# A two-layer attention and mixture-of-experts kernel: the end of each attention group put in another order, and the first expert's weight parts made at other places

## The chip, the cores and the metric

The kernel runs on one core of a Trainium2 chip. The metric is the device time of the whole program in microseconds; lower is better. Engines are called by the names of the profile: PE is TensorE, DVE is VectorE, ACT is ScalarE, POOL is GpSimd, SP is SyncE, which here only issues DMAs.

## What is computed

Two layers over 2048 tokens of 256 features (two batches of 1024), all fp32. Each layer is a cross-attention to 154 context rows and a mixture of eight experts of which every token takes two. The change lies wholly in the first layer.

```python
x = x + L0_attention(layernorm(x), ctx)   # 16 heads of 16, masked softmax over 154 keys, then @ wo + bo
# L0 experts, on xn = layernorm(x):
logits = xn @ gate_w.T
top_v, top_i = top_k(logits, 2)
probs = softmax(top_v)
for e in range(8):                        # wg, wu: 1024 x 256, wd: 256 x 1024
    hidden = silu(xn @ wg[e].T) * (xn @ wu[e].T)
    out += combine[e][:, None] * (hidden @ wd[e].T)
x = x + out
x = x + L1_attention(...)                 # one head, with an additive term
x = x + L1_experts(...)                   # the same with a capacity, gelu, I = 512
```

## The kernel before

Every engine runs an instruction stream of its own, written out by hand; semaphores (`S(name)`) tie them together. Nothing is scheduled by a tool, so an instruction's place in the code is its place in its engine's queue, and an instruction that waits holds everything behind it on that engine. A fp32 number that must be multiplied exactly is kept as two fp16 numbers, a high part and a low part; one engine casts to make the high part, another subtracts to make the low part.

**First attention.** The tokens are taken in `NG` = 4 groups of 512, numbered 0 to 3. A group goes through 20 steps `u` (16 heads, and 4 for the keys past 128). In each, TensorE makes scores in one of two PSUM banks (`score`), ScalarE takes their exponential into a ring of four tiles (L1120, `expo`) and casts it to the high part (L1123), and VectorE subtracts to get the low part (L1623, `probs`). Between these steps lie the maxima of the next group, and what remains of the previous group: its output projection (`turn_out`, `project_out`), the residual (`update`), the moments of the rows, and their transposition for routing (`turn_rows`, `rows_turned`).

**End of a group.** When all 20 low parts are there (`a0_plo`), TensorE weighs the values tile by tile (`weigh_values`, four tiles), ScalarE copies the low sums of each tile (`low_outputs`, L1098) and VectorE adds and divides (`head_outputs`, L1474 to L1478). In the same place the previous group is routed: TensorE makes its logits (`route_rows`, 16 fp32 matmuls), VectorE picks the two experts (`choose`, from L1509 on), ScalarE takes one exponential (`gates`) and writes the normalised rows (`normalise_rows`, L1070), TensorE counts positions (`route_positions`), and VectorE works out the row numbers in the experts' buffer (`place`). GpSimd splits the normalised rows into high and low fp16 parts (`split_rows`, L606 and L608, four tiles of each) and sends them with eight indirect DMAs to the DRAM buffer `rows` (`scatter`, L591).

**To the first expert.** After group 3 comes what is left: its own routing, the table of blocks (`count`, `table` set at L1609), the last two groups' `split_rows` and `scatter`, and the clearing of padding rows in `rows` (`clear_padding`). ScalarE then issues the load of the first block of rows (`load`, L1179), TensorE transposes it (L887) and the experts start. The scatters of all four groups, the first cleared block and the six low weight parts of expert 0 must be done by then.

**Weights of the first expert.** Its weights are six chunks of 128 x 1024 fp32, fetched by SyncE into three staging buffers (`fetch`, L412). ScalarE writes the high part of a chunk (`high_part`, L1063, tile `slot`), and before the change GpSimd the low part (`low_parts`, L546). A staging buffer is fetched again when its low part is done (`w_ready0`). Later experts' low parts are made by VectorE inside the blocks (`low_part`, L1692). The weights lie over tiles of the attention: the low parts of chunks 0 to 3 over the stacked queries of the even groups.

## Time and profile before

| | us |
|---|---|
| time before, median of 3 runs | 980.56 (978.98 to 983.68) |
| the profiled execution's own time | 974.74 |
| its span | 973.0 |
| PE busy | 733.2 (75%) |
| DVE busy | 549.4 (56%) |
| ACT busy | 401.9 (41%) |
| POOL busy | 331.2 (34%) |

The span runs from the first to the last instruction of the profiled execution. A busy share is a mean over the whole span, in which the first attention takes about the first quarter and the two mixtures of experts most of the rest, so it does not say what bounds a stage. The mean granted TensorE clock is 0.867 of full speed.

### The profile page before, as it was taken

Reading aid. Unit: us, or ns where it says so; the run is one execution under the profiler, and the core shown is the slowest. Engines: PE = TensorE matmul, PEld = TensorE weight load, DVE = VectorE, ACT = ScalarE, POOL = GpSimd, SP = SyncE. Lnnn points to the kernel's source line nnn. Section 1 sums busy time; section 2 is a strip of 40 time slices with the busy share of each in tenths; the row PEclk is TensorE's granted clock in tenths of the full one; section 3 lists DMA queues with packets and bytes.
Section 4 is the critical chain, followed back from the end, with each engine's and each line's share of the span. In section 5 each row is a group of like instructions: output and inputs, shape, how many; then the busy total and the mean of one; then the engine's idle time right before and its main releaser. Section 6 shows DMA issues by size and latency. Waiting matters only on the chain.

```text
span 973.0 us, 19222 instructions
## 1 busy us (share of the span) xinstructions
PE 733.2 (75%) x6314; PEld 573.8 (59%) x6315; DVE 549.4 (56%) x1360; ACT 401.9 (41%) x720; POOL 331.2 (34%) x322
## 2 busy tenths in 40 slices
PE   5567877884806999999979899977883287778882
PEld 4223535462705888888867788855542166657772
DVE  7786776868532555465645564676537054454441
ACT  1147464658213435454454453343411043444331
POOL 7326002338170122221321222444456322333332
PEclk9799897978756999999988999987555599999997
DMA  4651205104343524353435443142312444452232
GB/s 130 130 119 38 50 0 142 66 1 164 106 165 96 141 33 120 77 156 101 90 110 151 86 118 74 32 154 77 97 71 91 154 103 109 116 115 45 45 60 37
DMA packets 67985, 91.68 MB, mean 94 GB/s; under 512 B 14283, under 2 KB 54020, under 8 KB 67933
## 3 DMA queue, kind: packets, MB, share of 16 engines
q1 hardware_dynamic: 41372, 63.11, 21.5%
q0 software_dynamic: 14592, 16.24, 9.9%
q10 hardware_dynamic: 11968, 11.72, 4.6%
q8 instruction: 24, 0.39, 0.2%
q14 instruction: 29, 0.23, 0.1%
HBM read 63.94 MB, written 29.87 MB: 96 GB/s over the span
## 4 chain that ended last, share of the span: by engine, by line
PE 49%; DVE 21%; issue 12%; ACT 8%; POOL 4%; DMA 3%; ACTq 2%; DVEq 0%; POOLq 0%; SPq 0%
PE ps L640 46%; DVE probs L1623 3%; DVE probs L1707 3%; DVE mx L1486 2%; POOL rows L591 2%; DVE probs L1692 2%; ACT probs L1123 1%; DVE keys L1702 1%; DVE stats L1318 1%; DVE keys L1678 1%; DVE slot L1692 1%; ACT expo L1120 1%; ACT slot L1063 1%; ACT xln L1070 1%; ACT probs L1063 1%
## 5 line engine op out<-in xcount | busy, mean ns | idle before, releaser
L1702 DVE TENSOR_TENSOR keys<-probs,ps 128x512 f32<-128x512 f32 x122 | 83.2, 687 | 210.7 <-PE ps L640 160.5
L640 PE MATMUL ps<-keys,slot 128*128 128x256 f16 (+1 forms) x1440 | 151.8, 269 | 20.2 <-issue 10.9
L640 PE MATMUL ps<-keys,probs 128*128 128x256 f16 (+1 forms) x1488 | 141.5, 257 | 21.1 <-issue 16.1
L640 PEld LDWEIGHTS ps<-keys,slot 128*128 128x128 f16 x1440 | 130.3, 101 | 40.5 <-issue 20.9
L640 PEld LDWEIGHTS ps<-keys,probs 128*128 128x128 f16 x1488 | 124.6, 99 | 36.9 <-issue 21.5
L560 POOL DMA_INDIRECT attended<-keys,row_to x42 | 69.6, 1656 | 172.5 <-ACT keys L1205 166.1
L1193 ACT ACTIVATE probs<-ps 128x512 f32<-128x512 f32 x122 | 71.9, 598 | 88.4 <-PE ps L640 86.6
L1205 ACT ACTIVATE keys<-ps,carried 128x256 f32<-128x256 f32 x80 | 33.5, 470 | 161.1 <-issue 74.8
L1707 DVE TENSOR_TENSOR probs<-keys,probs 128x512 f16<-128x512 f32 x122 | 88.2, 724 | 3.0 <-ACT probs L1197 1.1
L1197 ACT CAST probs<-keys 128x512 f16<-128x512 f32 x122 | 74.9, 614 | 29.8 <-DVE keys L1702 28.8
L560 POOL DMA_INDIRECT out_x<-keys,row_to x38 | 59.1, 1556 | 70.4 <-ACT keys L1205 63.5
L1623 DVE TENSOR_TENSOR probs<-expo,probs 128x512 f16<-128x512 f32 x80 | 63.9, 811 | 32.9 <-ACT probs L1123 32.7
L640 PE MATMUL ps<-slot,probs 128*128 128x256 f16 x636 | 73.8, 273 | 10.1 <-DVE probs L1707 10.1
L640 PE MATMUL ps<-probs 128*128 128x256 f16 x612 | 71.3, 273 | 10.5 <-DVE probs L1707 10.5
L640 PEld LDWEIGHTS ps<-slot,probs 128*128 128x128 f16 x636 | 60.2, 98 | 20.4 <-DVE probs L1707 13.8
L640 PEld LDWEIGHTS ps<-probs 128*128 128x128 f16 x612 | 57.5, 98 | 20.8 <-DVE probs L1707 14.2
L1120 ACT ACTIVATE expo<-ps 128x512 f32<-128x512 f32 x80 | 47.8, 600 | 43.3 <-PE ps L640 41.1
L887 PE MATMUL ps<-identh,probs 128*128 128x128 f16 x336 | 26.5, 223 | 50.8 <-DMA probs<-rows 50.6
L556 POOL COPY row_to<-carried 128x2 int32 x40 | 11.8, 296 | 149.7 <-DMA attended<-keys,row_to 52.8
L887 PEld LDWEIGHTS ps<-identh,probs 128*128 128x128 f16 x336 | 21.9, 100 | 52.9 <-issue 50.3
L1678 DVE COPY keys<-ps 128x1024 f16<-128x1024 f16 x42 | 28.7, 684 | 43.1 <-PE ps L887 43.1
L1123 ACT CAST probs<-expo 128x512 f16<-128x512 f32 x80 | 49.0, 618 | 0.0
(256 smaller groups left out, 1238.7 us busy)
## 6 DMA issues: line engine op xcount, KB each, us to landing
inbox<-in_W SPq DMA_DIRECT2D x24, 512.0 KB, 4.3
probs<-rows ACTq DMA_DIRECT2D x44, 260.0 KB
inbox<-in_wg SPq DMA_DIRECT2D x16, 512.0 KB, 4.2
inbox<-in_wu SPq DMA_DIRECT2D x16, 512.0 KB, 4.9
inbox<-in_wd SPq DMA_DIRECT2D x16, 512.0 KB, 3.6
rows<-zeros SPq DMA_DIRECT2D x16, 260.0 KB, 2.4
x<-in_x SPq DMA_DIRECT2D x4, 512.0 KB, 6.6
q_out<-queries SPq DMA_DIRECT2D x8, 256.0 KB, 2.1
```

Source lines behind the costliest of these rows:

```text
L560: pool.indirect_dma_start(out=l.sums, out_offset=bass.IndirectOffsetOnAxis(ap=row_to[:, hf:hf + 1], axis=0), in_=yb[:, hf, :], in_offset=N ...
L640: return pe.matmul(o, l, r, start=start, stop=stop, **kw)
L887: last = pe.transpose(psh[:, 6, part * BLK + hf * P:part * BLK + (hf + 1) * P], x_raw[:, hf, part * P:(part + 1) * P], identh[:, :])
L1120: act.activation(e_ring[:, u % 4, :], ps[:, 4 + u % 2, :], ACT.Exp, scale=float(DK) ** -0.5).then_inc(S("a0_exp"), 1)
L1123: act.copy(p_hi[:, u - 1, :], e_ring[:, (u - 1) % 4, :]).then_inc(S("a0_phi"), 1)
L1193: act.activation(s_act[:, j % 2, :], ps[:, 2 * (j % 2), :], l.act).then_inc(S(r + "_s"), 1)
L1197: act.copy(h_hi[:, 2 * j - 2:2 * j, :].rearrange("p c t -> p (c t)"), h32[:, (j - 1) % 2, :]).then_inc(S(r + "_hh"), 1)
L1205: ins = act.activation(yb[:, hf, :], ps[:, 4 + hf, 0:D], ACT.Identity, scale=carried[:, bass.ds(g, 1), hf, 0:1].rearrange("p b d -> p (b d)"))
L1623: dve.tensor_tensor(p_lo[:, u, :], e_ring[:, u % 4, :], p_hi[:, u, :], ALU.subtract).then_inc(S("a0_plo"), 1)
L1678: dve.tensor_copy(xbT[:, :, :, :].rearrange("p a b c -> p (a b c)"), psh[:, 6, :]).then_inc(S(r + "_xbT"), 1)
L1702: dve.tensor_tensor(h32[:, j % 2, :], s_act[:, j % 2, :], ps[:, 2 * (j % 2) + 1, :], ALU.mult).then_inc(S(r + "_h32"), 1)
L1707: dve.tensor_tensor(h_lo[:, 2 * j - 2:2 * j, :].rearrange("p c t -> p (c t)"), h32[:, (j - 1) % 2, :], h_hi[:, 2 * j - 2:2 * j, :].rearran ...
```

## The change

In the first attention, at the end of each group, four things of the previous group's routing change places: the logits (`route_rows`) stand ahead of the first `weigh_values`; `choose` stands between the first and the second `head_outputs`; `gates` stands behind the first `low_outputs` and `normalise_rows` ahead of it; `route_positions` and `place` of the previous group stand ahead of the last tile instead of behind it or, for `place`, in the next group. The high parts of the first expert's weights are made in two threes: chunks 0 to 2 within group 2 (steps 4, 7 and 9) and chunks 3 to 5 behind the last group's gates, where all six were within group 3. The low parts of chunks 0 to 2 are made by GpSimd behind the scatter of group 1 (with a wait for group 2's scores), and those of chunks 3 to 5 by VectorE behind the table. SyncE fetches the second expert's first chunks behind the cleared padding.

```diff
--- before.py
+++ after.py
@@ -433,14 +433,16 @@
             for g in range(NG - 1):
                 sp.wait_ge(S("a0_x"), 2 * (g + 1))
                 keep_rows(L[0], g, "r0_kept")
-            for n in range(STAGES, k0 + STAGES):
-                fetch(L[0], n // k0, n % k0)
+            for n in range(STAGES, k0):
+                fetch(L[0], 0, n)
 
             sp.wait_ge(S("a0_st"), 20 * NG)
             sp.dma_start(phi[:, :, :], a["phi"].rearrange("(t p) s -> p t s", p=P)).then_inc(S("ld_phi"), 16)
             sp.wait_ge(S("a0_x"), 2 * NG)
             keep_rows(L[0], NG - 1, "r0_kept")
             clear_padding(L[0])
+            for n in range(STAGES):
+                fetch(L[0], 1, n)
             for b in range(B):
                 sp.dma_start(ctx1[:, b], a["ctxT"][b].rearrange("(k p) s -> p k s", p=P)).then_inc(S("ld_kv1"), 16)
             for n in ("Wk", "Wv"):
@@ -613,11 +615,10 @@
             spread_bias()
             for g in range(NG):
                 split_rows(L[0], g)
-                if g == 1:
-                    low_parts(L[0], 0, 0, range(0, STAGES))
                 scatter(L[0], g)
                 if g == 1:
-                    low_parts(L[0], 0, 0, range(STAGES, 2 * STAGES))
+                    pool.wait_ge(S("a0_st"), 20 * (NG - 1))
+                    low_parts(L[0], 0, 0, range(0, STAGES))
             rest_of_experts(L[0])
 
             low_parts(L[1], 0, 0, range(len(L[1].chunks)))
@@ -851,20 +852,20 @@
                             for kc in range(KC):
                                 last = mm(ps[:, 6, n * E:(n + 1) * E], mean[:, :], gate[:, n, kc, :], kc == 0, kc == 1)
                         last.then_inc(S("kv_ps"), 1)
+                if g:
+                    route_rows(g - 1, range(GT), g)
                 weigh_values(g, 0)
                 weigh_values(g, 1)
-                if g:
-                    route_rows(g - 1, range(GT), g)
                 if more:
                     turn_max(g + 1)
                 else:
                     turn_out(g, 0)
                 weigh_values(g, 2)
+                if g:
+                    route_positions(L[0], g - 1)
                 if not more:
                     project_out(g, 0)
                 weigh_values(g, 3)
-                if g:
-                    route_positions(L[0], g - 1)
             turn_out(NG - 1, 1)
             pe.wait_ge(S("a0_oev"), 4 * NG - 1)
             turn_rows(NG - 1, range(0, 2), 4)
@@ -1136,9 +1137,13 @@
                         q_parts(g + 2)
                     if g and u == 18:
                         rows_turned(g - 1, range(GT), 6, g)
-                    if g == NG - 1 and u in (4, 6, 8, 15, 17, 19):
-                        high_part(L[0], 0, 0, (4, 6, 8, 15, 17, 19).index(u))
+                    if g == NG - 2 and u in (4, 7, 9):
+                        high_part(L[0], 0, 0, (4, 7, 9).index(u))
+                    if g and u == 20:
+                        normalise_rows(g - 1)
                 low_outputs(g, 0)
+                if g:
+                    gates(L[0], g - 1)
                 low_outputs(g, 1)
                 if more:
                     maxima_turned(g + 1)
@@ -1146,16 +1151,14 @@
                     out_turned(g, 0)
                 low_outputs(g, 2)
                 low_outputs(g, 3)
-                if g:
-                    gates(L[0], g - 1)
                 if not more:
                     out_turned(g, 1)
-                if g:
-                    normalise_rows(g - 1)
             rows_turned(NG - 1, range(0, 2), 4, NG)
             rows_turned(NG - 1, range(2, GT), 4, NG + 1)
             normalise_rows(NG - 1)
             gates(L[0], NG - 1)
+            for n in range(STAGES, len(L[0].chunks)):
+                high_part(L[0], 0, 0, n)
 
             act.wait_ge(S("ld_w"), 4 * 16)
             act.wait_ge(S("a0_plo"), 20 * NG)
@@ -1616,8 +1619,6 @@
             q_low(1)
             for g in range(NG):
                 more = g + 1 < NG
-                if g >= 2:
-                    place(L[0], g - 2)
                 for u in range(20):
                     dve.wait_ge(S("a0_phi"), 20 * g + u + 1)
                     dve.tensor_tensor(p_lo[:, u, :], e_ring[:, u % 4, :], p_hi[:, u, :], ALU.subtract).then_inc(S("a0_plo"), 1)
@@ -1649,16 +1650,17 @@
                     if g + 2 < NG and u == 18:
                         q_low(g + 2)
                 head_outputs(g, 0)
-                head_outputs(g, 1)
                 if g:
                     choose(L[0], g - 1)
+                head_outputs(g, 1)
                 head_outputs(g, 2)
+                if g:
+                    place(L[0], g - 1)
                 if not more:
                     update(g, 0)
                 head_outputs(g, 3)
             dve.wait_ge(S("a0_x"), 2 * NG - 1)
             moments("r0", (NG - 1) * GT, 2)
-            place(L[0], NG - 2)
             update(NG - 1, 1)
             dve.wait_ge(S("a0_x"), 2 * NG)
             moments("r0", (NG - 1) * GT + 2, 2)
@@ -1727,6 +1729,9 @@
                         with dve.Fori(first, end) as g:
                             one_block(g)
 
+                if l.n == 0:
+                    for n in range(STAGES, len(l.chunks)):
+                        low_part(0, 0, n)
                 turned(0)
                 with dve.Fori(0, E // l.slots - 1) as pr:
                     for slot in range(l.slots):
```

Three places of the engines' queues follow. The names are the tiles that an instruction writes and reads: `probs` the low and high parts of the exponentials, `heads` the head outputs, `edge` the next group's maxima, `ev` the gates' exponential, `xln` the normalised rows, `lg` the logits, `slot` and `inbox` the first expert's weights and their staging.

ScalarE, end of group 2 and start of group 3, before:

```order
L1123 CAST probs<-expo 128x512 x2
L1098 COPY heads<-ps 128x256 x2
L1102 COPY edge<-ps 32x512
L1098 COPY heads<-ps 128x256 x2
L1057 ACTIVATE ev<-dv 128x4
L1070 ACTIVATE xln<-x,nb_r,ry_r 128x256 x4
L1120 ACTIVATE expo<-ps 128x512 x2
```

and after:

```order
L1124 CAST probs<-expo 128x512 x2
L1071 ACTIVATE xln<-x,nb_r,ry_r 128x256 x4
L1099 COPY heads<-ps 128x256
L1058 ACTIVATE ev<-dv 128x4
L1099 COPY heads<-ps 128x256
L1103 COPY edge<-ps 32x512
L1099 COPY heads<-ps 128x256 x2
L1121 ACTIVATE expo<-ps 128x512 x2
```

The four normalisations (`xln`) went from behind the last of four head copies to ahead of the first, and the gates' exponential (`ev`) from behind the fourth to behind the first; the exponentials of group 3 (`expo`) now follow the last head copy.

VectorE, at the same end of group 2, before:

```order
L1623 TENSOR_TENSOR probs<-expo,probs 128x512 x5
L1474 TENSOR_TENSOR heads<-ps,heads 128x256
L1475 RECIPROCAL rden<-ps 128x16
L1478 TENSOR_TENSOR heads<-heads,rden 128x256
L1474 TENSOR_TENSOR heads<-ps,heads 128x256
L1475 RECIPROCAL rden<-ps 128x16
L1478 TENSOR_TENSOR heads<-heads,rden 128x256
L1509 COPY lg<-ps 128x32
```

and after:

```order
L1624 TENSOR_TENSOR probs<-expo,probs 128x512 x5
L1477 TENSOR_TENSOR heads<-ps,heads 128x256
L1478 RECIPROCAL rden<-ps 128x16
L1481 TENSOR_TENSOR heads<-heads,rden 128x256
L1512 COPY lg<-ps 128x32
L1522 MAX mx<-lg 128x8 x4
L1525 MAX_INDEX ix<-mx,lg 128x8 x4
```

The logits' copy (`lg`), with which `choose` begins, moved from behind two head outputs to behind one.

GpSimd, from the end of group 1's rows to group 2's, before:

```order
L606 CAST penalties<-xln 128x256
L608 TENSOR_TENSOR penalties<-xln,penalties 128x256
L546 TENSOR_TENSOR slot<-inbox,slot 128x1024 x3
L591 DMA rows<-penalties,slot_s 18432x260 x8
L546 TENSOR_TENSOR slot<-inbox,slot 128x1024 x3
L603 IOTA xp 128x4
L606 CAST xp<-xln 128x256
```

and after:

```order
L608 CAST penalties<-xln 128x256
L610 TENSOR_TENSOR penalties<-xln,penalties 128x256
L593 DMA rows<-penalties,slot_s 18432x260 x8
L548 TENSOR_TENSOR slot<-inbox,slot 128x1024 x3
L605 IOTA xp 128x4
L608 CAST xp<-xln 128x256
L610 TENSOR_TENSOR xp<-xln,xp 128x256
```

The three weight subtractions that stood ahead of group 1's eight scatters stand behind them, and the other three are gone from this queue.

VectorE, from the end of the table to the experts, before:

```order
L1609 TENSOR_TENSOR table<-queries 1x26
L1610 TENSOR_REDUCE expert_of<-blk_passed 128x26
L1678 COPY keys<-ps 128x1024
L1681 SCALAR_TENSOR_TENSOR share<-probs,expert_of 128x2
L1683 COPY carried<-probs 128x2
L1685 TENSOR_TENSOR carried<-share,probs 128x2
L1731 UNCONDITIONAL_BRANCH
L1731 ISA
```

and after:

```order
L1612 TENSOR_TENSOR table<-queries 1x26
L1613 TENSOR_REDUCE expert_of<-blk_passed 128x26
L1694 TENSOR_TENSOR slot<-inbox,slot 128x1024 x3
L1680 COPY keys<-ps 128x1024
L1683 SCALAR_TENSOR_TENSOR share<-probs,expert_of 128x2
L1685 COPY carried<-probs 128x2
L1687 TENSOR_TENSOR carried<-share,probs 128x2
L1736 UNCONDITIONAL_BRANCH
```

Three subtractions of weights now stand between the table and the copy (`keys<-ps`) that hands TensorE the first block.

## Rows read from the trace of the kernel before

**Rows 1.** TensorE by time: start, length, line, op, tiles [idle before <-releaser]
```profile
150.07 0.60 PE L640 MATMUL ps<-v_ext,probs 128*128 128x33 f16 x16 [6.41 <-DVE probs L1623]
...
153.15 3.56 PE L640 MATMUL ps<-gate,xT 128*128 128x8 f32 x16
...
160.43 0.55 PE L640 MATMUL ps<-slot,keys 128*128 128x512 f16 x1
...
263.83 1.06 PE L640 MATMUL ps<-gate,xT 128*128 128x8 f32 x8 [0.23 <-ACT xT L1082]
...
299.75 1.01 PE L887 MATMUL ps<-identh,probs 128*128 128x128 f16 x8 [27.02 <-DMA probs<-rows]
```

**Rows 2.** Chain of waits, 195 to 305 us: start, length, what
```profile
291.48 4.25 DMA rows<-penalties,slot_s
```

**Rows 3.** GpSimd by time, same columns
```profile
225.66 1.28 POOL L591 DMA_INDIRECT rows<-penalties,slot_s  x1 [0.16 <-issue]
...
236.90 6.30 POOL L546 TENSOR_TENSOR slot<-inbox,slot 128x1024 f16<-128x1024 f32 x3
...
261.90 0.43 POOL L606 CAST xp<-xln 128x256 f16<-128x256 f32 x1 [18.61 <-ACT xln L1070]
...
267.17 1.02 POOL L591 DMA_INDIRECT rows<-xp,slot_s  x1 [0.80 <-POOL xp L608]
...
276.20 0.97 POOL L591 DMA_INDIRECT rows<-xp,slot_s  x1 [0.30 <-issue]
...
282.49 1.02 POOL L591 DMA_INDIRECT rows<-penalties,slot_s  x1 [0.80 <-POOL penalties L608]
```

**Rows 4.** ScalarE by time, same columns
```profile
145.33 1.03 ACT L1082 COPY xT<-ps 128x1024 f32<-128x1024 f32 x1
...
160.87 2.07 ACT L1070 ACTIVATE xln<-x,nb_r,ry_r 128x256 f32<-128x256 f32 x4
162.84 1.06 ACT L1120 ACTIVATE expo<-ps 128x512 f32<-128x512 f32 x2
...
210.26 1.06 ACT L1120 ACTIVATE expo<-ps 128x512 f32<-128x512 f32 x2
...
232.96 1.04 ACT L1063 CAST slot<-inbox 128x1024 f16<-128x1024 f32 x1 [2.52 <-DMA inbox<-in_wu]
...
240.69 0.65 ACT L1123 CAST probs<-expo 128x512 f16<-128x512 f32 x1
```

**Rows 5.** VectorE by time, same columns
```profile
152.24 0.42 DVE L1474 TENSOR_TENSOR heads<-ps,heads 128x256 f32<-128x256 f32 x1 [2.23 <-ACT heads L1098]
...
152.86 0.42 DVE L1478 TENSOR_TENSOR heads<-heads,rden 128x256 f32<-128x256 f32 x1
...
156.75 0.19 DVE L1509 COPY lg<-ps 128x32 f32<-128x32 f32 x1 [1.91 <-PE ps L640]
...
161.86 0.21 DVE L1547 TENSOR_TENSOR ohp<-oh,ps 128x64 f32<-128x64 f32 x1
...
164.44 0.69 DVE L1623 TENSOR_TENSOR probs<-expo,probs 128x512 f16<-128x512 f32 x1 [0.90 <-ACT probs L1123]
...
238.00 6.96 DVE L1623 TENSOR_TENSOR probs<-expo,probs 128x512 f16<-128x512 f32 x3 [1.26 <-ACT probs L1123]
...
272.32 0.17 DVE L1567 TENSOR_TENSOR penalties<-dn,penalties 128x4 f32<-128x4 f32 x1
...
276.95 0.17 DVE L1609 TENSOR_TENSOR table<-queries 1x26 int32<-1x26 f32 x1
...
318.56 1.22 DVE L1692 TENSOR_TENSOR probs<-inbox,probs 128x1024 f16<-128x1024 f32 x1
```

**Rows 6.** Windows: PE, PEld, DVE, ACT, POOL busy, granted clock, DMA share, GB/s
```profile
150.00:160.00 10.00, 9.93 (x177) 9.72 (x178) 5.01 (x31) 1.69 (x4) 0.00 (x0) 0.50 0.87 172
160.00:197.00 37.00, 29.31 (x161) 15.14 (x158) 31.33 (x72) 25.60 (x49) 14.10 (x17) 0.96 0.23 83
```

**Rows 7.** SyncE's DMA issues by time
```profile
278.10 12.22 SPq L418 DMA_DIRECT2D rows<-zeros  x8
```


## The prediction

> **What bounds the kernel now.** I read the chain of waits first, to see which stretch of the program is open to this change, then the four engines by time around the end of each attention group. The change touches only the stretch from group 1's end at 150 us to the first expert's first transposition at 299.75 us; the experts behind it keep their code, so what is won or lost is the shift of that transposition. It waited 27.02 us for the first block of rows [rows 1]. The chain shows what that block waited for: the last of GpSimd's indirect DMAs, issued at 291.48, which took 4.25 us to land [rows 2], and then the load. So GpSimd's queue sets the end. It was late twice. It got group 2's normalised rows only at 261.90, after 18.61 us of idleness ended by ScalarE's normalisation [rows 3], though the last exponential had been cast at 241.34 [rows 4] and VectorE's last low part was done at 244.96 [rows 5]. And from there it did two rounds in a row: eight scatters start at 267.17, the next eight at 282.49, 15.32 us for one round of scatter and split [rows 3].
>
> Ahead of that, two things stretch group 3. ScalarE casts six weight chunks in it, and for one it stood 2.52 us waiting for a DMA [rows 4]. GpSimd's three subtractions of 6.30 us at 236.90 [rows 3] lie on VectorE's last three low parts, which took 6.96 us where one alone takes 0.69 [rows 5]: 4.9 us lost. At the end of groups 1 and 2, TensorE's logits for the previous group stand between the second and third tile (3.56 us) [rows 1], and ScalarE's four normalisations (2.07 us) stand ahead of the next group's first exponential [rows 4].
>
> **The change, part by part.** All times below count from the moment when a group's last low part is done.
>
> *Logits and normalisation in the waiting time (groups 1 and 2).* TensorE sat idle for 6.41 us before 150.07 [rows 1]. The transposed rows it needs for the logits were there at 146.36 [rows 4], so 3.56 us of logits end at 149.92, only just hidden; in group 2 I allow 0.5 us of overhang. The normalisations go into ScalarE's own idle time behind its last cast; they hide under the wait for the first tile. What gets longer is VectorE's part: `choose` now stands between two head outputs. Its length: from 156.75 to 161.86 are 5.11 us, less two head outputs (1.04 each: 0.62 to the third instruction and 0.42 for it) and a 0.5 us wait between them: 2.53 us [rows 5]. The new path to the next group's first exponential: a tile's matmuls 1.54 (two in 150.07 to 153.15 [rows 1]), ScalarE's copy until 152.24, 0.63, head output 1.04, `choose` 2.53, the part of the next head output that frees the bank 0.62 [rows 5], the last tile 1.54, and 1.0 for the next group's first score (an estimate; its first matmul is 0.55 [rows 1]): 8.9 us. Before it was 162.84 - 150.07 = 12.8 [rows 1, 4], so 3.9 less. VectorE still has `place` (164.44 less 0.90 idle less 161.86 = 1.68 [rows 5]) and one head output behind the last tile, which gives its first low part at 7.9 (8.9 without the score) + 1.68 + 1.04 = 10.6 against 14.4 before. I take 3.7 us for group 1 and 3.7 - 0.5 = 3.2 for group 2: **6.9 us**. Bounds: nothing, if `choose` is held up by GpSimd's splitting, which now runs beside it, and 2 x 3.9 plus what the clock may give (below).
>
> *Three high parts in group 2.* ScalarE is busy 25.60 of 37.00 us there and VectorE 31.33 [rows 6]. Three casts of 1.04 us [rows 4] fit into its 11.4 us of idle time. I count nothing; without that cover it would be 3.1 us.
>
> *Group 3.* ScalarE went from 210.26 to 241.34, 31.1 us, with six casts (6.2) and a DMA wait (2.5) in it [rows 4]: 22.4 without. Three things come in. TensorE's two projections of the previous group, which the casts covered, now hold up the scores: 1.5 us each is my estimate, 3 in all (bounds 0 and 5.7, half of ScalarE's idle time in group 2, where they already do [rows 6]). GpSimd's three low parts now stand behind group 1's scatter: group 2's last low part came at 210.26 - 12.8 = 197.5 [rows 4], now 3.2 earlier, and `place` is done 9.6 later, at 203.9; the eight DMAs took 225.66 to 236.90, 11.2 us, so they run from about 215 to 221.6 [rows 3], in the middle of the group. VectorE stands for 6.30 less one low part, 5.6 us; the ring of four exponentials lets ScalarE run on for about three steps, so 3 us of it arrive (bounds 0 and 5.6; I take the middle, since VectorE's moments of the previous group come right behind and it must catch up). And 0.7 for the last low part. Sum 29.1 against 244.96 - 210.26 = 34.7: **5.6 us**. The last low part of all thus comes at about 244.96 - 12.5 = 232.5.
>
> *From there to the last scatter.* Group 2's rows are normalised right behind the last cast, so GpSimd splits them beside the first tiles, and only the slots bind: tile 1.54, copy 0.63, head output 1.04, `choose` 2.53, head output 1.04 (6.8), then group 3's `turn_out` 0.6, tile 1.54, copy 0.63, head output 1.04 and `place` 1.68: 12.3 us [rows 1, 5]. With 0.5 to start, the scatter begins at 12.8, the last one 15.32 later at 28.1; before, it began at 282.49 - 244.96 = 37.5 [rows 3, 5]. **9.4 us.** The floor under it is group 3's own slots. They were done at 272.49, 27.5 us behind the last low part, and the table at 277.12, 32.2 behind it [rows 5]. The slots are 0.6 us ahead of the new scatter: a further gain on GpSimd would find VectorE's chain there.
>
> *Weights behind the table.* Three casts of 1.04 and three subtractions of 1.22 us [rows 4, 5] end about 4 us behind the table, at 269, and the first block would be loaded at about 279. Ten us cover them. But VectorE's subtractions now run beside the last scatter. One of GpSimd's DMA instructions took 1.28 at 225.66, beside VectorE's low parts of group 3, and 0.97 at 276.20 [rows 3]; I take 0.5 us, bounds 0 and 3 x 1.22. SyncE's clearing of padding (12.22 us for eight issues [rows 7]) ends at about 278 instead of 290.3, so the first load now runs beside the last of it and the second expert's first three fetches. I take 1 us, bounds 0 and 4.
>
> Sum: 6.9 + 5.6 + 9.4 - 1.5 = **20.4 us**. I take 20. The profiled execution took 974.7 us, so it would be 954.7; the median of the runs is 5.8 us above it, so the forecast for the median is 980.6 - 20 = 960.5, rounded to 960.
>
> **A rule weighed against the trace.** TensorE's granted clock was 0.50 from 150 to 160 us [rows 6], behind those 6.41 us of idleness: its lower level, 1.2 GHz. Sixteen logit matmuls took 3.56 there and eight took 1.06 at 263.83 [rows 1], so the stretch runs at about 1.7 times the time it could. The logits now fill most of that gap. The Trainium skill, page "TensorE: Matmul & The Clock Gate", section on why this matters for kernels, says that throughput drops behind idle gaps between bursts and that one should leave none; by it the clock would stay up. If the clock stays at its upper level through the ends, a tile falls from 1.54 to about 0.95, 2 x 0.6 us at each of two ends, and at the last end three tiles and one projection, 2.5: 4.9 us more at most. The forecast goes without it, since 6.41 - 3.71 = 2.7 us stay idle ahead of the logits (150.07 less 146.36 is 3.71) and these are narrow matmuls.
>
> **The rivals.**
> - *As summed* (55%): 16 to 23 us less, 957 to 964.
> - *The clock stays up* (14%): 24 to 25 us less, 956. Against it: after the change there is still a gap before each end.
> - *GpSimd's subtractions arrive in full* (20%): VectorE has its moments and roots right behind the locked stretch and never catches up within the group, and `choose` is slowed by the splitting beside it. All 5.6 us instead of 3, and 1.5 at each of three ends: 7 less gain, 967. For it speaks the row of 6.96 us. The Trainium skill, page "GPSIMD Engine Reference", section Key points, says that GpSimd shares its SBUF interfaces with VectorE and that instructions with two SBUF inputs contend; by it `choose` (small operands from SBUF) suffers, its reductions from PSUM don't.
> - *The gain is given back ahead of the second expert* (5%): its first three chunks were staged long before, and are now fetched behind the clearing, at 278. They are wanted some 10 us after the restart at 280. If they land late, up to 10 us go: 970.
> - *No change beyond 0.5%, or slower* (6%). Slower needs one thing: that the first expert waits for its own weights. Chunks 3 to 5 are fetched only behind group 2's residual copy, cast behind the gates and subtracted behind the table. It would decide from the point where they are ready later than 299.75, 30 us behind my 269; each us beyond adds one. A VectorE queue blocked on `w_hi` by a late DMA also holds the first block's copy. The DMA wait of 2.52 us is the only such delay in the rows [rows 4]; 35 us late would give some 985.
>
> **How the numbers follow.** 0.5% is 4.9 us, about what a measurement of this kernel can tell from none. The first four cases are all faster by more: 94%; I give 0.93, 0.04 to the same and 0.03 to slower. The range reaches from the clock case with the 1.5 us of contention and 2 of the projections at nothing (952) to the third rival's far side and the fourth (970).
>
> **What the profile would show.** Right: logits end before the first tile's matmuls in groups 1 and 2; the next group's first exponential comes 8.5 to 9.5 us behind the last low part; GpSimd's three subtractions stand at 215 to 222 with a low part of 3 to 6 us beside them; its split of group 2 ends before the slots; the last scatter begins near 261 and the first expert transposition near 279. Wrong: an end of a group not shorter than 12.8; group 3 longer than 31 us; the first block waiting for `w_ready0`; ScalarE waiting for staging in the first block of the experts.

## The result, and the profile after

The changed kernel takes 966.6 us (median; 964.5 to 969.8), the kernel before on the same chip 979.9: ratio 0.9875 (95% interval 0.9845 to 0.9906), 12 to 13 us less. The forecast was 20 less, 960 (952 to 970). The same kernel timed again on another chip gave 964.9 (960.6 to 965.2) against 978.1, ratio 0.9868 (0.983 to 0.9906). Both of its profiled executions are used here, since they differ at one place that matters: the first has a span of 968.1, the second 963.3. Times without a label are us; groups count from 0, while the expectations below count from one in words ("the fourth group" is group 3).

| stage | before | forecast | after, 1st | after, 2nd |
|---|---|---|---|---|
| last low part of group 1, in the span | 150.01 | same | 153.35 | 150.45 |
| from it to the next low part, group 1 | 14.43 | 10.7 | 10.46 | 11.95 |
| group 2, first to last low part | 32.99 | same | 32.98 | 32.97 |
| end of group 2, the same | 14.43 | 11.2 | 11.94 | 11.94 |
| group 3, first to last low part | 33.10 | 27.5 | 29.63 | 29.63 |
| last low part to start of last scatter | 37.53 | 28.1 | 35.72 | 32.34 |
| its eight DMA instructions | 9.96 | 10.5 | 11.86 | 11.86 |
| from there to the first expert's transposition | 7.30 | 8.3 | 6.25 | 6.28 |
| that transposition, in the span | 299.75 | 279.3 | 292.19 | 287.42 |
| first block, to the second transposition | 15.67 | same | 15.68 | 16.67 |
| from there to the end | 657.6 | same | 660.2 | 659.2 |

The first line is no effect of the change: it is 3 us later in one execution of the kernel and not in the other (153.0 to 153.4 in five of the fourteen profiles of this study, one of them of the old order, 149.5 to 150.6 in the rest). The last line runs from 657.6 to 662.2 over all of them, with the kernel before at its lowest. That takes 1.6 from the difference of the spans, which is 9.7 (973.0 to 963.3) where the medians differ by 13; and the profiled execution of before (974.7) was 4 to 9 shorter than its timed ones.

The first expert's transposition in the second profile, 12.3 earlier than in [rows 1], and then TensorE at the end of group 1, first profile: start, length, line, op [idle before <-releaser].

```profile
287.42 1.01 PE L888 MATMUL ps<-identh,probs 128*128 128x128 f16 x8 [18.76 <-DMA probs<-rows]
```

```profile
149.62 3.58 PE L641 MATMUL ps<-gate,xT 128*128 128x8 f32 x16 [2.76 <-ACT xT L1083]
153.41 0.61 PE L641 MATMUL ps<-v_ext,probs 128*128 128x33 f16 x16 [0.21 <-DVE probs L1624]
```

The logits lie in the wait for the last low part (153.35) and end 0.2 ahead of it. The granted clock is at its lower level from 148.9 to 159.1, and a tile's matmuls are as long as before. In the second profile it is at the upper level from 154.3 to 157.7 and low again until 161.1, so the next group's first scores run slowly: that end takes 11.95 instead of 10.46. The short one is in the four profiles of the new order that have the 3 us above, the long one in the eight that have not. VectorE and then GpSimd in group 3, first profile:

```profile
216.93 0.68 DVE L1624 TENSOR_TENSOR probs<-expo,probs 128x512 f16<-128x512 f32 x1
218.22 7.53 DVE L1624 TENSOR_TENSOR probs<-expo,probs 128x512 f16<-128x512 f32 x3 [0.60 <-ACT probs L1124]
```

```profile
217.67 6.30 POOL L548 TENSOR_TENSOR slot<-inbox,slot 128x1024 f16<-128x1024 f32 x3
...
251.62 1.02 POOL L593 DMA_INDIRECT rows<-xp,slot_s  x1 [8.77 <-DVE xp L1570]
...
268.03 0.40 POOL L608 CAST penalties<-xln 128x256 f16<-128x256 f32 x1 [6.28 <-ACT xln L1071]
...
274.08 1.02 POOL L593 DMA_INDIRECT rows<-penalties,slot_s  x1 [1.63 <-DVE penalties L1570]
275.41 1.09 POOL L593 DMA_INDIRECT rows<-penalties,slot_s  x1 [0.30 <-issue]
276.81 0.97 POOL L593 DMA_INDIRECT rows<-penalties,slot_s  x1 [0.30 <-issue]
278.08 1.76 POOL L593 DMA_INDIRECT rows<-penalties,slot_s  x1 [0.30 <-issue]
280.15 1.96 POOL L593 DMA_INDIRECT rows<-penalties,slot_s  x1 [0.30 <-issue]
```

Group 2's scatter starts 13.3 behind the last low part (238.36), near the forecast (12.8). But then GpSimd does not go straight on as in [rows 3]: it is idle for 6.28, and again 1.63 for the slots. It no longer sets the end; the chain ScalarE, TensorE, VectorE does. In the first profile that chain has one odd stop, a wait that no semaphore explains. ScalarE, the last tile's low output (L1098 before):

```profile
256.56 0.37 ACT L1099 COPY heads<-ps 128x256 f32<-128x256 f32 x1 [8.08 <-remote]
```

TensorE had finished that tile at 252.99, and VectorE had freed what the copy needs at 249.1: 3.6 us are left over. The second profile does not have it:

```profile
251.60 0.37 ACT L1099 COPY heads<-ps 128x256 f32<-128x256 f32 x1 [4.56 <-PE ps L641]
```

### The profile page after: what moved, and what is told of

Same layout as the page of the kernel before. It is cut to its first block, busy times and chain, and to the rows that moved or that the text cites. A ratio compares the mean times of both kernels' runs of the same rounds, so it can differ in the third digit from the quotient of the medians.

```text
span 968.1 us, 19223 instructions
## 1 busy us (share of the span) xinstructions
PE 742.9 (77%) x6314; PEld 576.9 (60%) x6315; DVE 550.2 (57%) x1363; ACT 402.3 (42%) x720; POOL 324.1 (33%) x319
## 4 chain that ended last, share of the span: by engine, by line
PE 50%; DVE 21%; issue 14%; ACT 8%; DMA 3%; ACTq 2%; POOL 1%; DVEq 0%; POOLq 0%; SPq 0%
PE ps L641 47%; DVE probs L1709 3%; DVE probs L1624 2%; DVE mx L1489 2%; DVE probs L1694 2%; DVE keys L1704 2%; ACT probs L1124 1%; ACT expo L1121 1%; ACT probs L1196 1%; PE ps L973 1%; DVE keys L1680 1%; DVE slot L1694 1%; DVE stats L1321 1%; ACT probs L1064 1%; ACTq L1181 1%
## 5 line engine op out<-in xcount | busy, mean ns | idle before, releaser
L1624 DVE TENSOR_TENSOR probs<-expo,probs 128x512 f16<-128x512 f32 x80 | 60.9, 773 | 33.5 <-ACT probs L1124 31.5
L888 PE MATMUL ps<-identh,probs 128*128 128x128 f16 x336 | 26.5, 223 | 43.1 <-DMA probs<-rows 42.8
L641 PE MATMUL ps<-penalties,identb 128*128 128x462 bf16 x96 | 34.8, 362 | 18.7 <-DVE mx L1489 8.1
```

The costliest lines, as they stand in the source:

```text
L641: return pe.matmul(o, l, r, start=start, stop=stop, **kw)
L888: last = pe.transpose(psh[:, 6, part * BLK + hf * P:part * BLK + (hf + 1) * P], x_raw[:, hf, part * P:(part + 1) * P], identh[:, :])
L1624: dve.tensor_tensor(p_lo[:, u, :], e_ring[:, u % 4, :], p_hi[:, u, :], ALU.subtract).then_inc(S("a0_plo"), 1)
```

## The experiments

**The two halves alone.** The order of the group ends without the weights, and the weights without the order.

> The new order at the groups' ends alone; the weight parts stand where they stood before. Theory 1 (the two parts of the change act side by side, and the order carries most of it): the ends of groups 1 and 2 are 4.0 and 2.5 us shorter as in the profile after, group 3 stays at 34.7 us, and the stretch from the last low part to the first expert's transposition is some 5 us shorter than the 54.8 of before if the ScalarE stall of the profile after is absent, 1 to 2 if it is there; 9 to 12 us below before in all. Theory 2 (the weights carry it; the order only moves waits): 4 us below before or less, since the shorter group ends come back as a longer group 3, in which GpSimd's six subtractions now meet more of VectorE's low parts.

> The weight parts at their new places alone; the order at the groups' ends is that of before. Theory 1: group 3 about 31.5 instead of 34.7 us, the last scatter 2 us longer beside VectorE's subtractions, nothing else; 0 to 3 us below before. Theory 2 (the weights carry the gain): 7 us or more below before.

Measured: order alone 970.5, ratio 0.9924 (0.9895 to 0.9953); weights alone 981.3, ratio 1.0015 (0.9988 to 1.0043). The order alone is 7 below before, between the two theories (9 to 12, or 4 and less), and the weights alone gain nothing that the runs can tell, where up to 3 was expected. The sum, 0.6%, is less than both together (1.25%), by little more than the intervals allow, and the runs are of different chips: that the halves help each other is likely, not shown. With the order alone group 3 keeps its six casts and takes 34.9 us from first exponential to last low part (before 34.7). With the weights alone it takes 32.3, but the last scatter starts 41.1 behind the last low part instead of 37.5: GpSimd is still the bound there, and VectorE's subtractions, from 280.44, lie on its splitting, which takes 7.3 instead of 4.4.

```profile
280.16 0.67 POOL L610 TENSOR_TENSOR penalties<-xln,penalties 128x256 f16<-128x256 f32 x1
280.77 1.39 POOL L608 CAST penalties<-xln 128x256 f16<-128x256 f32 x1
282.25 1.52 POOL L610 TENSOR_TENSOR penalties<-xln,penalties 128x256 f16<-128x256 f32 x1
```

Another 2.3 go behind the last scatter: 9.59 from its end to the first expert's transposition instead of 7.30. SyncE's loads, which the weights' part of the change puts behind the clearing, pass there: 2.25 MB on its queue in that stretch, against 0.92 before.

**GpSimd's low parts to VectorE, in group 3's gap.**

```diff
-                if g == 1:
-                    pool.wait_ge(S("a0_st"), 20 * (NG - 1))
-                    low_parts(L[0], 0, 0, range(0, STAGES))
                 head_outputs(g, 1)
+                if not more:
+                    for n in range(STAGES):
+                        first_low(n)
                 head_outputs(g, 2)
```

> The changed kernel, but the low parts of chunks 0 to 2 are made by VectorE in the last group's end, between its second and third head output, where it is idle for 3.2 us in the profile after, instead of by GpSimd in the middle of group 3. Theory 1 (the 7.5 us low part beside GpSimd's subtractions is what makes group 3 31.5 us long, through VectorE and through TensorE's lower clock behind it): group 3 takes 26 to 28 us, and the time is 4 to 5 us below the changed kernel. Theory 2 (group 3 is bound by TensorE's projections and ScalarE's 20 steps; the ring covers the stop): group 3 takes 30 us or more and the time is within 2 us of the changed kernel.

Measured: 965.2, ratio 0.9861 (0.9818 to 0.9905). Group 3 takes 26.5 from first exponential to last low part, against 31.5: so GpSimd's subtractions cost 5.0 there, not the 3 of the forecast. VectorE's three took 3.49 (at 241.04), where it had waited 3.16 for the third tile anyway: the third head output starts 0.57 behind ScalarE's copy instead of 0.41. The 4 to 5 us in the total did not come: the ratio is that of the change (0.9875) within the noise, and the last scatter starts 38.75 behind the last low part instead of 35.72 in the first profile (both have ScalarE's stop, below). 0.8 of these 3.0 are the logits, which in the shorter group end only at 234.10, behind the last low part (233.05): the first tile is copied 2.65 behind it instead of 1.83.

**VectorE's low parts behind the last scatter.**

```diff
                 if l.n == 0:
+                    for n in range(2):
+                        dve.wait_ge(S(f"{r}_scattered{n}"), 16 * NT * TOP // 2)
                     for n in range(STAGES, len(l.chunks)):
                         low_part(0, 0, n)
```

> The changed kernel, but VectorE's three low parts behind the table wait until all scatters have landed. Theory 1 (VectorE's subtractions stretch GpSimd's DMA instructions in the last scatter): its eight DMA instructions take 10.0 us from first start to last end instead of 11.9, the last scatter lands 1.9 us earlier, and the first transposition comes 1.9 us earlier; the subtractions then end about when the first block is there and cost 0 to 1 us: 1 to 2 us below the changed kernel. Theory 2 (the longer DMA instructions come from SyncE's clearing beside them): 11.9 us stay, and the time is 0 to 3 us above the changed kernel, because the subtractions now stand behind the load.

Measured: 967.8, ratio 0.9879 (0.9847 to 0.9911). The eight scatters took 10.1 (273.61 to 283.71), the same two at 0.97, so 1.8 of the 1.9 us that the last scatter had lost are VectorE's subtractions beside them, and not SyncE's clearing:

```profile
276.33 0.97 POOL L593 DMA_INDIRECT rows<-penalties,slot_s  x1 [0.30 <-issue]
277.61 0.97 POOL L593 DMA_INDIRECT rows<-penalties,slot_s  x1 [0.30 <-issue]
278.89 0.98 POOL L593 DMA_INDIRECT rows<-penalties,slot_s  x1 [0.30 <-issue]
```

The restart, as the first expert's transposition is called from here on, came 51.7 behind the last low part instead of 53.8, as expected. The total did not follow: the first expert block took 20.4 instead of 15.7 (below).

**ScalarE's stop.** It stood in all four profiles of the new order so far (7.4 to 8.96 us, at the same copy), beside group 2's scatters and a packet of the queue that carries instructions (q8 in the DMA views). Two kernels were to tell whose it is: one holds these scatters back, one moves ScalarE's stream on by 40 instructions.

```diff
+                if g == 2:
+                    pool.wait_ge(S("a0_olo"), 4 * NG)
                 scatter(L[0], g)
```

> The changed kernel with one wait more: GpSimd starts the third group's eight scatters only when ScalarE has copied the last tile's low output (it has 6.28 us of slack behind them, before it waits for the normalised rows at 268.03). ScalarE's stop of 8.08 us ahead of that copy at 256.56 fell beside the first four scatters (from 251.62), and its instruction fetch runs over DMA. Theory A, the stop is an instruction fetch drawn out by the scatters' DMA descriptors on GpSimd: the stop shrinks to the 4 us or so that ScalarE waits for TensorE, the copy starts at about 253.1, 3.5 us earlier, the scatters start right behind it, and the last scatter and the restart come 3 to 3.5 us earlier (restart about 49 to 51 us behind the last low part of group 3, where the changed kernel had 53.8). Theory B, the stop is a fetch of 7 to 8 us whoever else uses the DMA engines: the copy stays at 7 to 9 us of idleness, the scatters start 5 us later than before, still end inside GpSimd's slack, and the restart stays within 1 us of the changed kernel's 53.8.

```diff
             x_evac("a0", 1, xT, 4)
+            for n in range(40):
+                act.copy(spare[:, n:n + 1], nb["a0"][:, 0:1])
             act.wait_ge(S("a0_s_ps"), 12)
```

> The changed kernel with 40 one-element copies on ScalarE in the 11.6 us in which it stands idle ahead of 51.29, so that everything behind them stands 40 instructions later in its stream; nothing is added behind them. If ScalarE's stop belongs to a place in its instruction stream (a fetch of the next piece, of whatever duration), it moves away from the low output of the fourth group's last tile, about 40 instructions earlier in the work, into the fourth group's exponentials (last low part of group 4 later by up to 8 us), and the copy there comes 3.5 us earlier. If the stop belongs to that copy or to the scatters that start beside it (a semaphore held up by them), it stays at the same copy, with 7.4 to 9 us. The copies themselves take under 11 us of ScalarE, so group 1 starts within 0.5 us of the changed kernel.

Measured: 961.4 and 964.6 (ratios 0.9835, 0.9781 to 0.9889, and 0.9879, 0.9826 to 0.9932). The stop was gone in both: 4.55 us of idleness, ended by TensorE. That looked like an answer until the unedited kernel was profiled again:

> The changed kernel once more, unedited, on the chip of the two runs below. ScalarE's stop of 8.08 us ahead of the fourth group's last low output was there in the changed kernel and in three of its variants, and absent in three others, which were taken on another occasion. If the stop belongs to the kernel (its place in ScalarE's stream beside the third group's scatters), it is here again with 7 to 9 us, and the restart comes 53 to 54 us behind the last low part. If it belongs to the occasion, ScalarE waits only 4.5 us for TensorE there, and the restart comes about 50 us behind.

It has no stop either (4.56, above). So neither run says anything of the cause, and a place in the kernel is not enough for it: the same instructions have it in one execution and not in another. It seems to go with the occasion: all three kernels of the new order that were profiled together on the second occasion have it (and the first profile after), none of the six that came next, one whole and one in part of the last two. The weights alone, in the old order, do not have it on that same occasion. What makes it is open. A packet of the instruction queue starts in ScalarE's idle time in every one of these profiles, with a stop and without.

**All parts out of GpSimd's and the last scatter's way,** with and without the held scatters. Low parts 0 to 2 behind group 2's last head output, 3 to 5 in group 3's gap, high parts 3 to 5 on ScalarE ahead of `gates` there:

```diff
                 low_outputs(g, 0)
+                if not more:
+                    for n in range(STAGES, len(L[0].chunks)):
+                        high_part(L[0], 0, 0, n)
...
                 head_outputs(g, 3)
+                if g == NG - 2:
+                    for n in range(STAGES):
+                        first_low(n)
```

> All six weight parts are out of the last scatter's way and none is on GpSimd: VectorE subtracts parts 0 to 2 behind the last head output of the third group, and parts 3 to 5, fetched ahead of the third group's kept rows, behind the second head output of the fourth, their high parts made by ScalarE in its 3 us of idleness ahead of the gates there; the third group's scatters wait for the last low output as in the run above. By my theory (two sums of weight parts that collide with GpSimd's instructions, and the stop of ScalarE): the fourth group takes 26.5 to 28.5 us from first exponential to last low part instead of 31.5, the slots of the third group stay 13 us behind the last low part, the last scatter takes 10.0 us instead of 11.86, and the restart comes 48 to 51 us behind the last low part instead of 53.8: 7 to 10 us under the changed kernel together, about 958 us. By the rival (the time behind the last low part is set by TensorE's and ScalarE's own chain, and what is freed is waited out elsewhere) the restart keeps 53 us or more behind the last low part and the time is 962 to 965.

> The run with the weight parts in the gaps, without GpSimd's wait ahead of the third group's scatters. ScalarE's stream stands three instructions further on at the last low output than in the changed kernel, since the high parts lie ahead of it. Theory A (a fetch at a place of the stream, drawn out by scatters beside it): the scatters start at the slots again, about 245.5, and the fetch falls about three instructions earlier, around 240 to 245, half beside them: a stop of between 4.5 (TensorE's own wait) and 9 us, restart 49.7 to 54 us behind the last low part of the fourth group, which comes 26.5 us behind that group's first exponential as with the wait. Rival (the stop does not depend on the scatters): the same time as with the wait, restart 49.7 us behind, within 0.5 us.

Measured: 961.9 (ratio 0.9855, 0.9799 to 0.9911) and 961.9 (0.9855, 0.9816 to 0.9894), the latter beside the 964.9 of the unedited change. As expected group 3 takes 26.5 and 26.6, the last scatter 10.1, and the restart comes 49.7 and 49.9 behind the last low part, at 281.3 and 282.0 of the span, 5.5 to 6.2 ahead of the second profile of the change. But the spans are only 4.0 and 3.6 shorter. What is missing stands right behind the restart. TensorE without the held scatters, and then in the second profile of the change:

```profile
284.87 3.95 PE L639 MATMUL ps<-keys,slot 128*128 128x256 f16 x23 [1.90 <-issue]
290.82 9.80 PE L639 MATMUL ps<-keys,slot 128*128 128x256 f16 x73 [2.00 <-issue]
```

```profile
290.10 4.67 PE L641 MATMUL ps<-keys,slot 128*128 128x256 f16 x23 [1.67 <-DVE keys L1680]
296.11 8.14 PE L641 MATMUL ps<-keys,slot 128*128 128x256 f16 x73 [1.34 <-issue]
```

Before, the 96 matmuls of this step run without a break (13.15 us from 302.43). Now they stop after 23 and for no semaphore. What the DMA queues carry in the first 12 us of the block, before:

```profile
DMA packets 274, 0.30 MB, mean 25 GB/s; under 512 B 16, under 2 KB 272, under 8 KB 272
q10 hardware_dynamic: 272, 0.27, 9.0%
q8 instruction: 2, 0.03, 1.2%
```

and with the parts in the gaps and the held scatters, from 281 to 293 of the span:

```profile
q1 hardware_dynamic: 2151, 2.95, 77.6%
q10 hardware_dynamic: 272, 0.27, 6.4%
q8 instruction: 2, 0.03, 1.0%
```

SyncE's loads (the second expert's parts, which the change put behind the clearing, and the second attention's inputs) now lie on the first block. The first block took 15.7 before and 15.2 and 15.1 in the two halves alone, 14.6 in the run below that restarts at 292.8; 16.7 in the change when it restarts at 287.4, 18.8 and 18.5 here, 17.3 in the last run, 15.8 to 16.1 in four others, and 20.4 in the one with the lows behind the scatter. The packets of the instruction queue are as many in both, but they come later. Ten of the fourteen profiles have the stop, from 0.3 to 2.9 long and always behind the 23rd matmul, and in all ten TensorE goes on 2.2 to 2.5 after the start of a packet of 16 KB on that queue (q8), the first behind the restart. In the four without it (before, the two halves alone, and the run below that restarts at 292.8) this packet starts 2.6 to 4.5 ahead of the 24th matmul. It starts 0.3 to 1.7 behind the block's first matmul where 0 to 1.25 MB of SyncE's loads pass in the 12 us behind the restart, and 2.8 to 4.4 behind where 2.5 to 2.9 MB do. So the stop is, by the profiles, a wait for instructions that are fetched late beside these loads; no run moved the loads alone. The granted clock can fall with the stop, which makes it dearer. With the lows behind the scatter the stop is 2.91, and behind it 28 matmuls run at the lower clock, 0.21 apart instead of 0.11, 2.8 more (window, busy time of PE, PEld, DVE, ACT and POOL, granted clock, DMA share, GB/s):

```profile
299.00:305.00 6.00, 5.83 (x28) 4.00 (x28) 0.99 (x2) 2.05 (x3) 0.00 (x0) 0.50 0.24 67
```

**The scatters held longer,** until ScalarE has copied the last turned output (`a0_oT`).

> The changed kernel with GpSimd's third scatter held until ScalarE has copied the last turned output (about 3 us later than in the run that waited for the last low output). Theory A: ScalarE waits 4.5 us for TensorE at the last low output, no stop of 7 us anywhere behind it, and the scatters, 10.1 us long from about 254.5, end at 264.6 at the latest, about 2 us ahead of the normalised rows (262.1 to 264.2 in that run, first row at 262.7), so up to 2 us may be lost at the last rows' split: the restart comes 50 to 52 us behind the last low part, the time is 1 to 4 us under the run of the unedited change. Rival (the stop belongs to the instruction's place alone or to the occasion): the stop is here exactly when it is in the unedited change.

Measured: 967.9, ratio 0.9903 (0.9865 to 0.9941): 3 slower than the unedited change, where 1 to 4 faster was expected. The scatters ended at 266.2, and group 3's rows, normalised at 264.2, were split only then, so the last scatter starts at 271.94, 33.7 behind the last low part instead of 32.3. That is 1.4; another 2.9 lie behind this scatter, 9.15 to the restart instead of 6.28, and as with the weights alone SyncE's loads pass there, 2.04 MB instead of 1.08. Then the first block runs without a stop, at 14.6. (Its profile is one of the five with 3 us more at the start.) The run has a use of its own: here GpSimd's splitting is not beside VectorE's choice. VectorE in this run, and in the second profile of the change:

```profile
263.29 0.16 DVE L1531 TENSOR_TENSOR dv<-dv,ry_r 128x4 f32<-128x4 f32 x1
...
263.96 0.24 DVE L1539 TENSOR_TENSOR sel<-oh 128x32 f32<-128x32 f32 x1
...
264.56 0.17 DVE L1544 TENSOR_TENSOR cumb<-cumb,gsum 128x8 bf16<-128x8 bf16 x1
```

```profile
263.74 0.66 DVE L1529 TENSOR_TENSOR dv<-dv,ry_r 128x4 f32<-128x4 f32 x1
...
264.85 0.68 DVE L1537 TENSOR_TENSOR sel<-oh 128x32 f32<-128x32 f32 x1
...
266.00 0.59 DVE L1542 TENSOR_TENSOR cumb<-cumb,gsum 128x8 bf16<-128x8 bf16 x1
```

From the logits' copy to the slots it takes 4.08 here, 5.49 in the change, 3.76 before.

**The choice behind the second head output,** in group 3 alone: on the changed kernel, and together with the parts out of the way (low parts 3 to 5 now ahead of the last update).

```diff
-                if g:
+                if g and more:
                     choose(L[0], g - 1)
                 head_outputs(g, 1)
+                if not more:
+                    choose(L[0], g - 1)
                 head_outputs(g, 2)
```

> The changed kernel with one step put back in the fourth group alone: VectorE chooses for the third group behind the second head output instead of ahead of it (and ScalarE's gates follow the second low output). In the repeated run of the change TensorE waits 3.70 us there and turns the outputs 7.03 us behind the last low part; its later pieces run at the low clock (a transposition of 1.02 instead of 0.66, a projection of 2.04 instead of 1.13 us), and the last slots come 30.9 us behind. My account of the missing gain: about 2.6 us is the choice standing ahead of the turned outputs, 1.2 the clock, 1.7 the choice slowed by GpSimd's split beside it. By it the outputs are turned 4.3 to 4.6 us behind the last low part, the last slots come 28.2 to 28.5 behind if TensorE's clock stays low and 27 if it rises with the shorter idleness, the last scatter starts 29.6 or 28.4 behind instead of 32.3, and the restart comes 2.5 to 4 us sooner. Rival (the chain is bound by something behind it, the turned positions or GpSimd): the outputs are turned earlier, but the last slots come 30 us or more behind.

> The step of the run above together with all parts out of GpSimd's and the last scatter's way: high parts 3 to 5 on ScalarE ahead of the second low output of the fourth group, their low parts on VectorE ahead of the last update, where it stood idle 4.03 us, parts 0 to 2 behind the third group's last output. No wait of GpSimd is added. By my account both gains add up: fourth group 26.5 us from first exponential to last low part, last scatter 26.5 to 30 us behind it and 10.1 long, restart 44 to 47.5 us behind the last low part (49.9 without this step), at 276.5 to 279.5 us of the span where the early part runs as in the repeated run; about 957 to 959 us. Rival: the last update is delayed by the low parts ahead of it (3.5 us of work in 4 of idleness, which shrinks when TensorE's clock rises), and the restart comes 48 us or more behind.

Measured: 964.5, ratio 0.9854 (0.983 to 0.9879), and 962.0, ratio 0.984 (0.9816 to 0.9864), both within the noise of the change. TensorE and ScalarE in the first of them:

```profile
240.88 1.11 PE L761 MATMUL ps<-ident,heads 128*128 128x128 f32 x4 [1.55 <-DVE heads L1483]
...
250.71 0.66 PE L761 MATMUL ps<-ident,heads 128*128 128x128 f32 x4 [2.94 <-DVE heads L1483]
```

```profile
249.20 0.37 ACT L1099 COPY heads<-ps 128x256 f32<-128x256 f32 x1 [5.25 <-PE ps L641]
...
258.67 0.59 ACT L1083 COPY xT<-ps 128x512 f32<-128x512 f32 x1 [6.19 <-PE ps L783]
```

The outputs are turned 4.9 behind the last low part instead of 7.0, and TensorE waits 1.55 instead of 3.70. But ScalarE copies the last tile 1.4 late (matmuls done at 247.76) and the turned rows 1.2 late (257.45), and TensorE's clock falls again in the projections. The restart comes 49.9 behind instead of 50.5. The first step of my account holds and the gain did not arrive. The two delays look like the stop that comes and goes, so the run doesn't price the choice. In the combined run ScalarE's high parts held up the second low output (turned 6.8 behind) and the stop came in full (7.48 ahead of the copy at 247.67): restart 51.1 behind, where 44 to 47.5 was expected. It is no faster than the runs without this step.

## Why the prediction was off

The direction, the range and the bound that was expected to move were right, and the size was not: 12 to 13 us instead of 20. The median fell outside the 957 to 964 of the likeliest case, and one of the prediction's own signs of being wrong came: group 3 took 31.5 where it was to take no more than 31. The list below rests on these rows besides those above: where ScalarE and TensorE stood in group 3 (first profile after), and two pieces of TensorE's work behind it, in the second profile after and then before.

```profile
224.63 0.60 ACT L1121 ACTIVATE expo<-ps 128x512 f32<-128x512 f32 x1 [3.40 <-DVE probs L1624]
225.28 0.61 PE L641 MATMUL ps<-qs,keys 128*128 128x512 f16 x1 [3.68 <-ACT expo L1121]
```

```profile
253.11 1.02 PE L761 MATMUL ps<-ident,heads 128*128 128x128 f32 x4 [1.55 <-DVE heads L1481]
254.80 2.04 PE L641 MATMUL ps<-w_wo,heads 128*128 128x256 f32 x4
```

```profile
260.06 0.66 PE L760 MATMUL ps<-ident,heads 128*128 128x128 f32 x4 [1.43 <-DVE heads L1478]
261.39 1.13 PE L640 MATMUL ps<-w_wo,heads 128*128 128x256 f32 x4 [0.24 <-ACT heads L1088]
```

Step by step, on the second profile after:

- **Ends of groups 1 and 2:** 3.7 and 3.2 forecast, 2.5 and 2.5 measured (4.0 and 2.5 in the first profile). The new path is as forecast: the choice between two head outputs takes 2.54 (2.53 forecast), and in group 2 the logits end 0.8 behind the last low part (0.5 forecast). The miss is behind the last tile: the first score takes 1.5 at the low clock instead of the estimated 1.0, and ScalarE makes two exponentials ahead of its first cast, so that ScalarE and not VectorE sets the first low part (VectorE waits 1.66 and 1.30 for it). Group 1 differs between the profiles by the next group's first scores, 0.38 each in the first and 0.62 in the second, at the low clock.
- **High parts in group 2 cost nothing:** right to 0.02 us.
- **Group 3:** 5.6 forecast, 3.5 measured. Its other terms were right together: without GpSimd's low parts it took 26.5 against the 26.1 that the forecast has without them (22.4 + 3 + 0.7); no run takes them apart. **The step that failed is the choice of "3 us of it arrive", the middle between 0 and 5.6.** The run without them shows 5.0. ScalarE stood 3.40 us for VectorE's low parts, and TensorE, idle for 3.68, came back at the low clock.
- **Last low part to last scatter:** 9.4 forecast, 5.2 measured (1.8 in the first profile). This is the largest miss. The forecast saw the floor, group 3's own slots, 27.5 us behind the last low part, and **took it over from the profile before as if the change did not touch it**. They came 31.5 behind. By the profile 1.1 of it is the choice and its neighbours, which stand ahead of the turned outputs (the second turn starts 16.2 behind instead of 15.1); 1.3 TensorE's low clock, a transposition of 1.02 instead of 0.66 and a projection of 2.04 instead of 1.13; 1.7 the choice beside GpSimd's splitting, which now comes at the same moment. The last is shown: with the splitting elsewhere the choice is 1.4 shorter. The first two are read from the profiles. The run made to test the first was spoilt, though in the run with the held scatters, at the high clock, the last update comes 19.6 behind against 21.1 in the change and 18.7 before, which splits the 2.4 us in the same way. In the first profile ScalarE's stop of 3.6 comes on top.
- **Contention:** the last scatter lost 1.9 instead of 0.5, and the run that moves the low parts shows 1.8 of it. The clearing and the load lost nothing in the change, where 1.0 was allowed (7.30 fell to 6.28), but 2.3 more than before with the weights alone and 2.9 more than in the change in the run with the scatters held longer: SyncE's loads fall ahead of the restart or behind it. In the second profile they fall behind it, 1.0 us in the first block.

These add up: the restart came at 287.4 instead of 279.3, 8.1 late, made of 1.3 and 0.7 at the two ends, 2.1 in group 3, 4.2 up to the last scatter, 1.4 in it and 0.4 at the start, less 2.0 that the clearing and the load did not lose.

Of the rivals, "GpSimd's subtractions arrive in full", with its 967 at 20%, names two of the causes better than the likeliest case: nearly full collision in group 3 (5.0 of 5.6), and 1.7 for the choice beside the splitting, though at the last of its three ends only. They make 3.7 of the 7 that it takes away, so that its 967 lies near the result is in part luck. "The clock stays up" did not happen: TensorE waits 2.76 us ahead of the logits, and they were as long as before (3.58). By the Trainium skill, page "TensorE: Matmul & The Clock Gate", section on why this matters for kernels, filling the gap should have kept it; the trace does not bear that out for these narrow fp32 matmuls, which filled 3.6 of the 6.4 us. At the end of group 2 no idle time of TensorE is longer than 1.7 in the 15 us before, and the clock falls all the same, at 193.24 in the first profile, 0.9 into an idle time of 1.60. The other page of the Trainium skill that was weighed, "GPSIMD Engine Reference", section Key points, says that the two contend, and the traces agree in both directions: VectorE's three subtractions beside GpSimd's took 7.53, and GpSimd's cast beside VectorE's 1.39 instead of 0.40. GpSimd's DMA instructions, 1.76 and 1.96 instead of 0.97, are slowed as well.

## What to carry to other kernels

When a change takes the bound away from one engine, the floor under the gain is another chain, and its time in the old profile is only a floor if nothing of the change stands beside it: ask for each of its instructions what now runs at the same moment. Put two-input element-wise work of VectorE where GpSimd is idle, not where it computes or issues indirect DMAs; here three weight subtractions on GpSimd beside VectorE's low parts cost 5 us, and the same three on VectorE in a gap of nearly the same length 0.2. Loads that are moved later do not vanish: look at what they pass beside, the instruction queue too. And before explaining one long wait, profile the same kernel again.

## What the hardware showed

- ScalarE can stand 3.0 to 4.3 us longer than its semaphores ask (1.4 in one profile), at one copy, in some executions of a kernel and not in others. Its cause is open. A packet of the instruction queue passes nearby in all of them, but in those without a stop too.
- TensorE stops for 0.3 to 2.9 us in the first block of the experts when 2.5 to 2.9 MB of other loads pass there, and not at all when 0 to 1.25 MB do. It goes on 2.2 to 2.5 us after a 16 KB packet of the instruction queue has started, in ten profiles of ten.
- From the last scatter's end to the first expert's transposition it takes 9.2 and 9.6 us where 2.0 to 2.3 MB of SyncE's loads pass, 5.9 to 7.3 where 0.9 to 1.1 MB do.
- GpSimd's instruction for an indirect DMA, 0.97 us long, takes up to 1.96 beside a VectorE subtraction of 128 x 1024, and its cast 1.39 instead of 0.40. Small VectorE instructions of 0.16 to 0.19 take 0.59 to 0.68 beside GpSimd's splitting.
